# Latent attention with a residual: a third bank for the scores, the last unit normalised on chip, the low halves on GpSimd

## The reference, cut to what matters

```
xn     = (x - mean) / sqrt(var + 1e-5)
q      = xn Wq                  16 heads of 64
latent = xn Wkv_down            64 wide, shared by all heads
k, v   = latent Wk_up, latent Wv_up
attn   = softmax(causal(q k^T / 8));  y = attn v;  att = y Wout
ffn    = tanh(xn weight aux_weight1 aux_weight2 + bias)
out    = x + att + ffn
```

## Time and profile before

| | us |
|---|---|
| median of 3 runs | 1982.55 (1980.58 to 1983.97) |
| the profiled execution | 1996.93 |
| its span, first to last instruction | 1994.9 |
| TensorE busy | 1954.7 (98%) |
| GpSimd busy | 1479.2 (74%) |
| VectorE busy | 1338.2 (67%) |
| ScalarE busy | 1150.0 (58%) |

### The profile page before, as it was taken

One profiled execution on the slowest core, in us unless ns is written; L12 is line 12 of the kernel. 1 busy time (PEld: TensorE's weight loads), 2 busy tenths in 40 slices (PEclk: granted clock), 3 DMA queues, 4 the chain that ended last, 5 costly groups with the idle time before them and its releaser, 6 DMA issues.

```text
span 1994.9 us, 38740 instructions
## 1 busy us (share of the span) xinstructions
PE 1954.7 (98%) x13512; PEld 1314.3 (66%) x13512; DVE 1338.2 (67%) x3619; ACT 1150.0 (58%) x2203; POOL 1479.2 (74%) x1291
## 2 busy tenths in 40 slices
PE   8999999999999999999999999999999999999996
PEld 6666666666666666666666666666766666666653
DVE  5778666776567766587666866669666695665652
ACT  4555555656555565555656556555565556565552
POOL 0587688776877777786787778786777876878785
PEclk8999999999999999999999999999999999999997
DMA  4221112212213212222212122122122221122110
GB/s 131 49 78 49 48 49 65 76 50 62 52 44 88 58 42 60 57 76 54 53 43 79 54 55 64 43 79 52 52 60 60 68 55 49 52 65 55 50 41 25
DMA packets 117842, 116.77 MB, mean 59 GB/s; under 512 B 24208, under 2 KB 100880, under 8 KB 117648
## 3 DMA queue, kind: packets, MB, share of 16 engines
q1 hardware_dynamic: 117648, 114.29, 21.4%
HBM read 53.94 MB, written 8.91 MB: 32 GB/s over the span
## 4 chain that ended last, share of the span: by engine, by line
PE 86%; DVE 9%; issue 3%; ACT 1%; POOL 1%; DMA 0%; POOLq 0%; DVEq 0%; ACTq 0%; SPq 0%
PE ps L998 24%; PE ps L932 21%; PE ps L1012 13%; PE ps L980 12%; PE ps L983 11%; PE ps L1036 3%; DVE ps L1234 2%; DVE x_in L1320 2%; DVE split_lo L1255 1%; DVE maxima L1239 1%; PE ps L1025 1%; PE ps L1065 1%; POOL p_sum L1377 0%; DVE xT_lo L1332 0%; PE ps L809 0%
## 5 line engine op out<-in xcount | busy, mean ns | idle before, releaser
L1377 POOL TENSOR_TENSOR p_sum<-p_sum,probs 128x512 f32<-128x512 f32 x672 | 863.7, 1313 | 174.1 <-ACT probs L1142 173.3
L1142 ACT ACTIVATE probs<-ps 128x512 f32<-128x512 f32 x1152 | 667.4, 597 | 344.8 <-PE ps L983 322.3
L1234 DVE CUSTOM_DVE_ANT_0 ps<-ps,causal 128x512 f32<-128x512 f32 (+4 forms) x1024 | 520.1, 528 | 263.2 <-PE ps L1012 257.9
L998 PE MATMUL ps<-probs,latent 128*32 128x512 f32 x4608 | 522.8, 595 | 0.0
L1012 PE MATMUL ps<-k_hilo,q_hi 128*128 128x512 f32 (+4 forms) x1536 | 477.9, 356 | 11.2 <-DVE maxima L1234 4.8
L980 PE MATMUL ps<-q_hi,k_hilo 128*128 128x512 f32 x1152 | 474.4, 412 | 5.1 <-ACT probs L1142 3.6
L1239 DVE TENSOR_REDUCE maxima<-ps 128x1 f32<-128x512 f32 (+1 forms) x512 | 325.9, 637 | 205.2 <-PE ps L1012 201.7
L983 PE MATMUL ps<-q_lo,k_ones 65*128 65x512 f32 x1152 | 456.7, 396 | 0.0
L1377 POOL TENSOR_TENSOR p_sum<-probs 128x512 f32<-128x512 f32 x224 | 294.0, 1324 | 119.8 <-ACT probs L1142 119.6
L1012 PEld LDWEIGHTS ps<-k_hilo,q_hi 128*128 128x128 f32 x1536 | 283.1, 190 | 106.4 <-issue 24.2
L998 PEld LDWEIGHTS ps<-probs,latent 128*32 128x32 f32 x4608 | 136.6, 109 | 306.4 <-issue 302.1
(11 more groups left out here) (102 smaller groups left out, 2256.4 us busy)
## 6 DMA issues: line engine op xcount, KB each, us to landing
q_hi<-q_hi SPq DMA_DIRECT2D x256, 128.0 KB, 2.4
norm<-recips SPq DMA_DIRECT2D x256, 128.0 KB, 2.9
q_lo<-q_lo SPq DMA_DIRECT2D x128, 128.0 KB, 2.4
x_in<-in_L_attn_x_bld SPq DMA_DIRECT2D x16, 512.0 KB, 4.5
acc<-in_L_attn_x_bld SPq DMA_DIRECT2D x32, 256.0 KB, 3.1
out_x<-acc SPq DMA_DIRECT2D x64, 128.0 KB, 1.7
q_lo<-rows SPq DMA_DIRECT2D x128, 4.0 KB
rows<-norm SPq DMA_DIRECT2D x128, 4.0 KB
```

The costliest lines, as they stand in the source:

```text
L998: last = nc.tensor.matmul(y_bank[row:row + WIDTH, :], latent[par][:, key_block(unit, s), half:half + WIDTH], probs[:, t % PT_SLOTS, g * BA ...
L1142: nc.scalar.activation(probs[:, t % PT_SLOTS, g * BANK:(g + 1) * BANK], ps[:, bank_of[kind, key], :], ACT.Exp).then_inc(exp_done, 1)
L1234: nc.vector.tensor_tensor_reduce(bank, bank, causal[:, BANK - w:BANK], 1.0, LOWEST, ALU.add, ALU.max, maxima[:, unit % 4, h, 0:1]).then_in ...
L1377: nc.gpsimd.tensor_tensor(sums, other, probs[:, slot, part], ALU.add).then_inc(pool_done, 1)
```

## The change

Six things are changed together.

- **Banks.** `HOMES` lets scores use banks 0, 1 and 2, maxima 3, 4 and 2, and the small pieces (`MT`, `R`, `O`, `F`) 4 to 7 where they had 5 to 7.
- **The planner.** `BATCH` 6 becomes 8, `LEAD` 13 becomes 12, `MT` is due five steps earlier, and two conditions on when something late goes ahead of a score are changed.
- **The low halves.** `LO` goes from VectorE to GpSimd, for units 0 to 126.
- **The last unit's sums.** Unit 127 has no additions on GpSimd. After each of its steps `broadcast_sums` multiplies ones (128 by 32) with the exponents, over all 512 columns, four quadrants beside each other, into one bank of maxima; the last such group is its `R`.
- **The last unit's reciprocal.** The sums are then already on every partition. VectorE takes the reciprocal of each half bank of 256 columns straight from PSUM and multiplies (`DV`); ScalarE and VectorE split by halves (`HF`, `LF`). The copy, the four transfers and GpSimd's product are gone for this unit.
- **The first stage.** `fold wff` goes ahead of the last two maxima, and `MT 0` between the two parts of `Q (1, 0)`. The three loads of `acc` leave `load_all` and stand behind `QD (1, 0)`.

```diff
-HOMES = {"ST": (0, 1), "MAX": (2, 3, 4), "Y": (5, 6, 7), "P0": (5, 6, 7), "P1": (5, 6, 7)}
+HOMES = {"ST": (0, 1, 2), "MAX": (3, 4, 2), "Y": (5, 6, 7), "P0": (5, 6, 7), "P1": (4, 5, 6, 7)}
-LANDING = {"Q": 3500, "MT": 2300, "X": 7000, "XA": 5000, "RG": 3200, "RO": 2200, "RB": 5200}
+LANDING = {"Q": 3500, "MT": 2300, "X": 7000, "XA": 5000, "RG": 3200, "RO": 2200, "RB": 4600}
-BATCH = 6
+BATCH = 8
-LEAD = 13
+LEAD = 12
...
             elif kind == "LO":
-                self.normal[key] = self.run("DVE", when, DVE_TIME[kind])
+                self.normal[key] = self.run("POOL", when, (1300, 1350))
...
-                out.append((max(self.max_end[self.turns[0]] + LATER["MT"], bank), now - 4, self.place_mt))
+                out.append((max(self.max_end[self.turns[0]] + LATER["MT"], bank), now - 9, self.place_mt))
...
-            idle_act = self.free["ACT"] < now - 300
+            idle_act = self.free["ACT"] < now + 100
-            if late and (not st or step - late[1] > 1.0 or not idle_act):
+            if late and (not st or step - late[1] > 0.5 or not idle_act):
...
-    plan += [("W", "fold wvo"), *maxima[3:6], *two_parts("Q", (1, 0)), *maxima[6:]]
-    plan += [("W", "fold wff"), ("MT", 0), *two_parts("Q", (1, 1)), ("QL", (1, 0)), ("QD", (1, 0))]
+    plan += [("W", "fold wvo"), *maxima[3:6], ("W", "fold wff"), *maxima[6:]]
+    plan += [("Q0", (1, 0)), ("MT", 0), ("Q", (1, 0)), *two_parts("Q", (1, 1))]
+    plan += [("QL", (1, 0)), ("QD", (1, 0)), ("XA", 0), ("XA", 1), ("XA", 2)]
...
-            for use in range(RING):
-                sp.dma_start(acc[:, 2 * use:2 * use + 2, :], x_pair(use)).then_inc(acc_loaded[use], 16)
...
+            def broadcast_sums(t, start, stop):
+                for i in range(QUADRANTS):
+                    part = slice(i // 2 * BANK, (i // 2 + 1) * BANK)
+                    last = nc.tensor.matmul(ps[i * WIDTH:(i + 1) * WIDTH, bank_of["R", final], :],
+                                            ones[:, :], probs[:, t % PT_SLOTS, part],
+                                            start=start, stop=stop)
+                return last
...
                     last.then_inc(pv_done, 1)
+                    if unit == final and s < block_of(unit):
+                        if s == 0:
+                            take_bank("R", unit)
+                        broadcast_sums(t, s == 0, False)
...
+                elif kind == "HF":
+                    act.wait_ge(last_divided, 2 * part + 2)
+                    if part == 0:
+                        act.wait_ge(p1_full, count.p1("O", unit - SPLIT_SLOTS) + 1)
+                    nc.scalar.activation(split_hi[:, unit % SPLIT_SLOTS, half_bank(part)],
+                                         y[:, unit % Y_SLOTS, half_bank(part)],
+                                         ACT.Copy).then_inc(last_hi, 1)
...
+                elif kind == "DV":
+                    nc.vector.reciprocal(norm[:, slot, cols], ps[:, bank_of["R", unit], cols]
+                                         ).then_inc(last_divided, 1)
+                    dve.wait_ge(last_divided, 2 * part + 1)
+                    nc.vector.tensor_tensor(y[:, slot, cols], y[:, slot, cols], norm[:, slot, cols],
+                                            ALU.mult).then_inc(last_divided, 1)
+                elif kind == "LF":
+                    dve.wait_ge(last_hi, part + 1)
+                    nc.vector.tensor_tensor(split_lo[...], y[...], split_hi[...], ALU.subtract
+                                            ).then_inc(last_lo, 1)
...
+                elif kind == "LO":
+                    slot = key % SPLIT_SLOTS
+                    pool.wait_ge(norm_hi, key + 1)
+                    nc.gpsimd.tensor_tensor(split_lo[:, slot, :], y[:, key % Y_SLOTS, :],
+                                            split_hi[:, slot, :].bitcast(F32),
+                                            ALU.subtract).then_inc(norm_lo, 1)
...
+                if unit == final:
+                    continue
```

More of the change, by code:

```diff
@@ L253, in choices @@
         if "P1" in self.open:
-            out.append((0, now - 0.5, self.place_p1_half))
+            if self.open["P1"] < self.units - 1 or ("LF", 1) in self.split:
+                out.append((self.split.get(("LF", 1), 0), now - 0.5, self.place_p1_half))
         else:
@@ L348, in place_p1_half @@
         self.out[u] = done
+        for part in range(2):
+            if (u + 1, part) in self.multiplied:
+                self.after(max(done, self.multiplied[u + 1, part]) + part, "HF", (u + 1, part))
         if u + SPLIT_SLOTS in self.multiplied:
@@ L367, in place_r @@
         self.plan.append(("R", u))
+        if u == self.units - 1:
+            done = self.on_pe("R", ready, PE_TIME["PV"])
+            for part in range(2):
+                self.after(max(done, self.y_copied[u]) + part, "DV", (u, part))
+            return
         self.takes("P1", "R", u)
```

63 lines of the change are left out of this document (52 added, 11 removed).

## The result

| | before | after |
|---|---|---|
| runs, first series (five each) | 1982.55 us (1980.58 to 1983.97) | 1996.50 us (1993.69 to 2001.12) |
| the profiled execution, its span | 1996.93, 1994.9 | 1999.85, 1998.1 |

Runs against runs the changed kernel is slower here: ratio 1.0071, 95% interval 1.0055 to 1.0087. The forecast was 1971.0. (The table ahead of the prediction calls 1982.55 the median of 3 runs; it is of these five.) On two other chips the changed kernel came out at 0.9989 (0.9969 to 1.0009) and 1.0046 (1.0019 to 1.0072) of the kernel before, with single runs from 1979 to 2009 us. So even the sign hangs on something that differs from run to run, and the profile shows what. Medians and ratios leave out slow runs, more than 1.5% above the fastest of the same kernel, of which there are two, both in experiment 3.

A forecast was written before the change was run, and what follows sets the result against it. TensorE's queue was taken to set the time. Terms -7.3 -7.1 +4.0 -5.0 +7.7 -0.7 -3.2 gave -11.6 us, 1985.3 profiled, 1971.0 as median; own range 1965.5 to 1976.5 (chance 0.50), outer 1958 to 1989.

The forecast's parts named there:

- one more wait of 1.1 us in each of the seven batches, 7.7 us: VectorE's normalisation held up by a GpSimd with fewer gaps, TensorE waiting behind it: 7.7 us lost, bounds 0 and 21.
- The other terms: Tile changes -7.3, third bank -7.1, maxima +4.0, low halves -5.0, first stage -0.7, end -3.2 us; -19.3 together.
- The starved VectorE: Rival: GpSimd without gaps holds up VectorE's normalisation in seven batches; slower, 1989.9 us at 3.8 us a batch; chance 0.19.
- the last line of the sum: From profiled execution to median: 1985.3 us expected for the profiled one, the same 14.4 us difference as before gives 1971.0.
- The end: From the last PV group to the last addition: 20.3 us instead of 23.5, so 3.2 gained, bounds 4.8 and 1.8.
- The low half near the end: Low half at 1943 us: its 3.33 us TensorE wait and 1.7 us of half clock go, 5.0 gained, bounds 2 and 9.
- Tile changes: On TensorE, 114 groups of 32-column products instead of 139, at 0.29 us each: 7.3 us gained, bounds 5 and 8.
- third bank: Scores find their bank free more often, 120 fewer late starts at 0.06 us: 7.1 us gained, bounds 0 and 16.7.
- maxima: Maxima share bank 2 with scores, 144 tight places instead of 100: 4 us lost, bounds 0 and 12.
- GpSimd: Low halves added to GpSimd, 127 at 1.287 us: busy time from 1479 to about 1622 us, 82% of the span.
- The first stage: At the program's start, the first score comes earlier, near 51.3 us: 0.7 us gained, bounds 1.2 and a loss of 0.6.
- the thing named as late next: In the first stage, bank 0 is free only when VectorE has split wff, behind the split of Q (1, 0).

The follow-up runs named there:

- experiment 3: The changed kernel with VectorE's scalings of x_in as scalar_tensor_tensor, the scale a second input, in place of tensor_scalar: 1988.43 us over ten runs, ratio 0.9995.
- e3_ff_first: The changed kernel with the first scaling of x_in in each batch moved behind the two feed-forward additions to acc: 1979.55 us, ratio 0.9970.
- e1_after: The changed kernel run again with no edit, on the chip of the second series: 1987.38 us.
- e1_before: The kernel before, run and profiled again with no edit: 1987.11 us, ratio 0.9984.
- e5_after: The changed kernel run a third time with no edit: 1998.00 us, ratio 1.0046.
- e4_capped: The changed kernel with GpSimd waiting, three instructions behind each normalisation step's place, until VectorE has done that step: 1978.45 us, ratio 0.9959.

## Why the prediction was wrong

The step that failed is "one more wait of 1.1 us in each of the seven batches, 7.7 us". The mechanism was named; its size was read off the wrong thing. I priced the two waits that I saw behind the hold-up and bounded the term at 3 us a batch. What a hold-up costs is the batch's length with and without: 2.85 us before, 7.1 after. The profiled execution had four, 6.1 + 3 x 7.1 = 27.4 us. The profile that the sum starts from had four as well, at 2.85, together 11.4. So the term is 16.0 us, not 7.7.

The other terms were too large. Take the hold-ups out and the span after is 1970.7. `e3_ff_first`, which had none, has 1971.8. The other two profiles of the changed kernel come to 1970.6 and 1972.6 when their hold-ups are taken out (in `e1_after` the one of 7.3 us at another step, 6.5 us in the second batch) and their first mask is set to the same 50.97 us. The kernel before comes to 1983.5 (1994.9 - 11.4). So without hold-ups the change is worth 12 to 13 us, of which 1.5 to 2.5 are an earlier first mask; my sum without that term had 19.3. From profile to profile the sum said -11.6, and the span moved by +3.2: 8.3 us of the difference are the hold-ups and 6.5 the other terms.

Two things were missed. In the new order the first `LN4` stands between `F` and `FA` from the normalisation of the fourth batch on, which runs inside the third, and PV takes F's bank next; before it stood right behind `FA`. I had followed the maxima alone. And the count of hold-ups is not fixed by the order: 4, 0 and 3 in three profiles of one kernel. The starved VectorE, with a chance of 0.19, was the right rival, priced at 1989.9 for 3.8 us a batch. Measured are 27.4 / 7 = 3.9, but that the two agree is luck: four batches paid 6.1 to 7.1 us and three paid nothing, in this execution.

A second error lies in the last line of the sum, and it is the larger one. I took the 14.4 us between before's profile and its median as a shift to carry over. 11.4 of it is the length of four hold-ups, the very thing under debate, if the runs behind the median had none. The profile after lies 3.4 us above its median, so 11.0 of the 25.5 us between forecast and result are this shift.

Point by point, as far as the traces tell the terms apart:

- *The end:* -3.2 forecast, -2.1 measured (23.5 to 21.4). The rows after:

```profile
1973.62 1.07 PE L1044 MATMUL ps<-probs,latent 128*32 128x512 f32 x8
...
1984.06 0.39 PE L969 MATMUL ps<-wvo_hi,split_hi 128*128 128x256 f32 x1
...
1984.19 1.76 DVE L1319 RECIPROCAL norm<-ps 128x256 f32<-128x256 f32 x1 [11.45 <-PE ps L1002]
...
1987.97 0.36 PE L969 MATMUL ps<-wvo_hi,split_hi 128*128 128x256 f32 x1 [2.21 <-POOL split_lo L1438]
...
1991.70 0.55 PE L969 MATMUL ps<-wvo_hi,split_hi 128*128 128x256 f32 x1 [1.12 <-DVE split_lo L1327]
...
1994.64 0.42 DVE L1344 TENSOR_TENSOR acc<-acc,ps 128x256 f32<-128x256 f32 x1 [2.75 <-PE ps L969]
```

  The twelve groups took 10.4 us as counted. The reciprocal took 1.76, not 2.4. Behind the pause of 2.21 nearly all of both last output products ran at 1.2 GHz, which I had half assumed; with both at 1.2 GHz my sum was 21.7.
- *The low half near the end:* its wait of 3.3 us is gone and the clock is 1.00 where it was 0.83. The last batch as a whole went from 250.7 (`before`) to 239.3 us (`e3_ff_first`), -11.4, where the end and this term had -8.2: TensorE's waits in it for low halves, sums and exponents fell from 14.1 to 5.1 us, and the time at half clock from 20.0 to 6.8 us. But the first three batches went from 722.0 to 725.9 us, which I had not foreseen; the third alone is 3.4 us longer (242.8 for 239.4) with no wait of TensorE's products over 0.2 us. Together they give -7.5; that this comes near -8.2 is luck.
- *Tile changes, third bank, maxima:* -10.4 in the sum. A batch without hold-up went from 239.35 to 238.65, so the four steady ones gave 2.7 us. There are three groups fewer in each; at the 0.29 of the forecast that is 0.87, more than the 0.7. So nothing is left for the bank, though the waits for it went as forecast: 0.10 us a late start was too much. That a late load costs nothing where products are in flight is a guess; no run shows it by itself. The maxima did not get worse.
- *GpSimd:* 1579 busy, not 1620; its additions took 1290 ns instead of 1313. The low half took 1.29 as assumed. No TensorE wait for one stood in a steady batch; the three there are, up to 2.2 us, stand in the last.
- *The first stage:* first score at 49.28 instead of 52.00. Most of it is the clock, though: 4.9 us at 1.2 GHz stand ahead of the first mask, where before had 10.2. With the same time at 1.2 GHz the first mask comes at 58.66 (`e1_before`) and 58.05 (`e5_after`) for some 20.5 us, and at 53.43 (`before`) and 53.57 (`e4_capped`, the same first stage) for 10.2. So the gain is between nothing and 0.6, where 0.7 was forecast. The first score now waits for the split of `wff`, the thing named as late next.

```profile
49.28 0.56 PE L1026 MATMUL ps<-q_hi,k_hilo 128*128 128x512 f32 x1 [1.89 <-DVE wff_lo L936]
```

**What stays open.** Why VectorE is let in at the end of GpSimd's instruction in one execution and not in another. In the changed kernel VectorE comes 0.28 to 0.31 us behind the start of GpSimd's low half in both cases. And the scatter of `e3_ff_first` is not all explained: the first stage alone gives nearly 8 us (first mask at 51.0 to 58.7 over the profiles), and the rest was not profiled run by run. The median of the first series, too, is explained by one profiled run of its five.

## What to carry to other kernels

Price a disturbance by the length of a whole period with and without it, not by the waits that are listed behind it. Where an instruction can be held up for long, look at what stands behind it on its engine and which bank or slot that keeps; putting the short releases ahead of it cost nothing in a steady batch here (238.6 us), and the kernel with it ran 0.3% faster than the one before. And do not carry the distance between one profiled execution and a median over to another kernel before you know what it is made of. Parts of a schedule that were made for each other (groups, banks, the engine of a step) have no single prices: with one undone, this kernel was 0.7 to 3% slower than the one it started from.

## What the runs showed of the hardware

- VectorE's hold-up by GpSimd is not bounded by one instruction. In the five profiles of the two kernels there are twelve long hold-ups of the scaling (five of 7.64 to 7.65 us before; four, none and three of 9.68 to 9.69 after). They span eight back-to-back GpSimd instructions before and ten after, and each ended 0.15 us after GpSimd's last instruction before a gap of 4 us or more. The Trainium skill (SBUF — State Buffer, section "Who interferes with whom") has the other engine blocked for the whole of one instruction. The 1.15 us of the scaling in `e1_after`, let in at the end of the one instruction that was running, fit that; the 1.50 in `e1_before` are the last 0.08 us of one instruction and the whole of the next, and the long ones do not fit at all.
- The small steps of the normalisation, 8 columns wide, are held up alike: 4.8 us in five batches of each profile of the changed kernel, over four GpSimd instructions. They stand in every batch of 238.6 us too, so what they cost is not shown.
- `bn_stats`, which reads SBUF and writes 6 numbers, was not held up: with GpSimd busy all the time, 24 took 8.20 us, five times in each of the two runs with the delay, and none took over 0.43 us.
- TensorE's clock fell to 1.2 GHz with the pause of 4.3 us in the middle of full work (granted clock 0.67 from 905 to 912 us). It fell for a shorter time, too, where VectorE's delay left it two pauses of 0.87 and 0.68 us within 1.2 us: 0.94 over the 30 us around them. The 3.6 us of late maxima contain that.

```profile
905.00:935.00 30.00, 28.46 (x179) 20.80 (x179) 27.50 (x82) 16.36 (x32) 21.66 (x20) 0.94 0.16 40
```
